# A cond-layernorm attention block on one core: SP stores the finished rows, residuals are kept in DRAM early, and TensorE sums two slabs where GpSimd summed one

## The chip, the cores and the metric

The kernel runs on one core of a Trainium2 chip. Its metric is the device time of one execution in microseconds (us), given as the median of several runs. The engines are TensorE (PE; its weight loads are PEld), VectorE (DVE), ScalarE (ACT), GpSimd (POOL) and SyncE (SP), which here only issues DMAs. Each engine runs its own list of instructions in order, and semaphores tie the lists together.

## The reference

`x` has 4 batches of 1024 tokens of 512 channels; there are 16 heads of 32 channels.

```
def _sln(h, w, ...):                       # layernorm with a gain and a bias from cond
    ln = (h - mu) / jnp.sqrt(var + EPS) * ln_g + ln_b
    return (w @ Wg.T + bg)[:, None, :] * ln + (w @ Wb.T + bb)[:, None, :]
h = _sln(hidden, w, ...)
qkv = (h @ Wqkv.T + bqkv).reshape(B, N, num_heads, hd, 3)
energy = jnp.einsum('bhqd,bhkd->bhqk', q, k)
att = jax.nn.softmax(energy, axis=-1) / D ** 0.5
out = jnp.einsum('bhqk,bhkd->bhqd', att, v)  ->  (B, N, D)
h1 = (out @ Wp.T + bp) + hidden
return _sln(h1, w, ...) + h1
```

## The kernel before

The 64 heads (4 batches by 16) are worked in 16 iterations of 4 heads; the 4096 tokens are 16 pairs of 128-token tiles. Every engine has a hand-written program in which an iteration is 32 steps, 8 for each head: step = 8 s + k, s the head in the iteration, k = 0 to 7. What an engine does at a step stands in small tables (`PAIR_ADD_STEP`, `NORM_SCALE_STEP`, `OUT_LOW_STEP` and so on). A step has no clock: an engine comes to it when its own list and its waits let it.

**One head.** TensorE makes the plain scores (ps_a, ps_w, or one bank of ps_st; L821), of which VectorE takes row maxima (L1367, `half_max`); the negated maxima are turned (L815), copied (L1374, L1376, `max_rows`), and SP stores them as two more rows of `q_stack` (`store_row`, L511, at k = 5 of the head before). Then TensorE makes the turned scores with the maximum already taken off (L835, ps_st) and ScalarE takes exp of them into eight slabs of 128x1024 (L1130; `p`, and `p_far` for every second head once it is free). TensorE multiplies the slabs with V (`weighted`, L852) in two halves of four slabs. The first turned score of the next head needs the row of `store_row` and stands at k = 7.

**The sum of the exponentials.** Of each half of four slabs VectorE adds slab 0 to slab 1 (`slab_add`, L1294), POOL adds slab 2 to slab 3 (`pair_add` with even j, L1658) and then slab 1 to slab 3 (odd j, same line). TensorE multiplies the one slab that is left with a constant (`chain_sum`, L865), at k = 0 of the next head for the first half and at k = 4 for the second. SP carries the sums to `sum_t` (`store_sums`, L527, k = 7), VectorE inverts them at step 9 (L1288) and SP stores them at step 10 (L533).

**Three kinds of iteration.** Iterations 0 to 10 ("tiles") also norm and project a pair of x tiles for a later batch: POOL scales it (`norm_scale` with `power`, steps 15 and 20; L1511 to L1523) and gives it gain and bias (`norm_gain`, steps 16 and 24). Iterations 11 to 14 ("bare") have no x tiles left, and iteration 15 ("last") has a list of its own. From iteration 4 on, each iteration also finishes a pair of output tiles ("outs"): SP loads `go_s` (gain and bias), the attention rows and the scales at step 14 and x itself into `res_t` at step 1 (`load_residual`, L554); POOL adds bp to it (`residual`, L1549), scales the rows (`out_norm`, L1539) and makes their low part (`out_low`, L1544); TensorE projects (L726, in bare iterations at steps 25 to 31), VectorE adds residual and projection (`out_sum`, L1303), and POOL norms, scales and adds in `out_scale` and `out_finish` (L1558 to L1570). `out_finish` ends with the store of the rows from POOL's own queue (L1572), at steps 3 and 11 of the next iteration. SP waits for the second `out_finish` before it loads the next `go_s` (step 14; step 5 in the last iteration). SP's list is strictly in order, so what stands behind that wait waits too.

`power` is eps + variance, minus the mean (L1512), a drain, the -0.5 power, a drain.

Of the kernel before, what the change touches and what calls it, by code (L numbers as in the profile page):

```python
# [72 lines left out]
RESIDUAL_BARE = {15: 0, 16: 1}  # L73
# [8 lines left out]
OUT_LOAD_STEP = 14  # L82


def conditioned_attention(nc, x, cond, ln_g, ln_b, Wg, bg, Wb, bb, Wqkv, bqkv, Wp, bp, out):
    B, N, D = x.shape
    HD = 32
# [15 lines left out]
    out_rows = out.rearrange("b n d -> (b n) d")  # L103

# [5 lines left out]
    mark_d = nc.dram_tensor("mark_scratch", [2, 1, 16], F32, kind="Internal").ap()  # L110
# [8 lines left out]
    with ExitStack() as ctx:  # L119
# [121 lines left out]
        res_ready = sem("res_ready")  # L241
        scale_in = [sem(f"scale_in{s}") for s in range(2)]
# [33 lines left out]
        LATE = END - 1  # L276
        PRE_LOAD_STEP = {11 + 2 * t: t for t in range(8)}
# [6 lines left out]
        ACC_ADD_STEP = {9: (0, 1), 10: (2, 3), 20: (4,), 22: (5,), 24: (6,), 26: (7,)}  # L284
        LATE_MM_STEP = {10: 0, 12: 1}
# [102 lines left out]
        SUM_SLOT = [3, 7]  # L388

# [39 lines left out]
        def _(sp):  # L429
# [198 lines left out]
            def iteration(i, tiles, norms, outs, first=False, last=False, gather=False):  # L628
                pair = i - FIRST_OUTS
                for s in range(4):  # L630
                    u = 4 * i + s
                    for k in range(8):
# [34 lines left out]
                        if last and step == 5:  # L667
# [24 lines left out]
            with sp.Fori(1, FIRST_OUTS) as i:  # L692
                iteration(i, True, True, False)
            with sp.Fori(FIRST_OUTS, LAST_TILES - 1) as i:
# [24 lines left out]
        def _(pe):  # L719
# [137 lines left out]
            def chain_sum(g, s, h, near=False):  # L857
# [199 lines left out]
        def _(act):  # L1057
# [61 lines left out]
            def exps(i, step, paired, tiles, behind):  # L1119
# [3 lines left out]
                                2: (pair_added, 4 * v + 2 * half + 1), 3: (sum_done, 2 * v + half + 1)}[k % 4 if paired else 3]  # L1123
                for e in range(2):
# [18 lines left out]
            def iteration(i, mode, outs, first=False, more=False, joining=False):  # L1143
                pair = i - FIRST_OUTS
                tiles, last = mode == "tiles", mode == "last"
                for step in range(32):
# [12 lines left out]
                    exps(i, step, paired, tiles, 1 if tiles or (joining and s == 0) else 2)  # L1159
# [46 lines left out]
        def _(dve):  # L1206
# [89 lines left out]
            def out_sum(pair, a):  # L1296
# [3 lines left out]
                dve.wait_ge(res_ready, P + 1)  # L1300
# [111 lines left out]
            def iteration(i, mode, norms, outs, first=False, late=True, closing=False, joining=False):  # L1412
                pair = i - FIRST_OUTS
                tiles, last = mode == "tiles", mode == "last"
                for s in range(4):
                    for k in range(8):
# [32 lines left out]
                        if outs:  # L1449
                            for a in sums:  # L1450
                                out_sum(pair, a)
# [38 lines left out]
        def _(pool):  # L1490
# [15 lines left out]
            for a in range(2):  # L1506
                G.dma_start(mark_d[a], ident[0:1, 0:16]).then_inc(y_out[a], 16)
# [9 lines left out]
            def norm_scale(pair, a):  # L1517
# [5 lines left out]
                G.tensor_scalar(h_tile[:, a, :], x_tile[:, a, :], std_t[:, a, 0:1], std_t[:, a, 1:2], ALU.add, ALU.mult  # L1523
# [26 lines left out]

            def out_scale(pair, a, count, gains=None):

                pool.wait_ge(out_stat, 2 * pair + a + 1)

# [3 lines left out]
                G.tensor_scalar(y, h1_t[:, a, :], ostd_t[:, a, 0:1], ostd_t[:, a, 1:2], ALU.add, ALU.mult  # L1558
# [5 lines left out]
            def out_finish(pair, a, count):  # L1564
# [6 lines left out]
                pool.wait_ge(out_pool, count + 5)  # L1571
                G.dma_start(out_rows[bass.ds((2 * pair + a) * 128, 128), :], y).then_inc(y_out[a], 16)  # L1572
# [18 lines left out]
            def last_iteration(i):  # L1591

                count = 10 * LATE + ONE
                for step in range(32):
# [158 lines left out]
```

## Time and profile before

| | |
|---|---|
| time, median of 3 runs | 1386.43 us (1386.4 to 1388.2) |
| the profiled execution: its time / its span | 1391.84 us / 1390.2 us |
| PE / POOL / DVE / ACT busy, of the span | 93% / 76% / 77% / 51% |
| mean granted TensorE clock | 0.97 |

Times in the rows below are counted from the start of the span. Busy time of PE is of overlapping matmuls, so a busy PE is not PE at its peak. A clock of 1.00 is 2.4 GHz, of 0.50 it is 1.2 GHz. POOL's, DVE's and PE's lists run at different steps at one time.

### The profile page before, as it was taken

Reading aid. Unit: us, or ns where it says so; the run is one execution under the profiler, and the core shown is the slowest. Engines: PE = TensorE matmul, PEld = TensorE weight load, DVE = VectorE, ACT = ScalarE, POOL = GpSimd, SP = SyncE. Lnnn points to the kernel's source line nnn. Section 1 sums busy time; section 2 is a strip of 40 time slices with the busy share of each in tenths; the row PEclk is TensorE's granted clock in tenths of the full one; section 3 lists DMA queues with packets and bytes.
Section 4 is the critical chain, followed back from the end, with each engine's and each line's share of the span. In section 5 each row is a group of like instructions: output and inputs, shape, how many; then the busy total and the mean of one; then the engine's idle time right before and its main releaser. Section 6 shows DMA issues by size and latency. Waiting matters only on the chain.

```text
span 1390.2 us, 33206 instructions
## 1 busy us (share of the span) xinstructions
PE 1294.5 (93%) x9988; PEld 904.0 (65%) x9988; DVE 1065.7 (77%) x1754; ACT 702.4 (51%) x1374; POOL 1062.6 (76%) x755
## 2 busy tenths in 40 slices
PE   7898999999999999999999999999989898989993
PEld 4897676767676767676776767677545555555562
DVE  5345788888888888787888878787968788887535
ACT  4221355555565556455555556555545555555341
POOL 1444176767676799899898999997897989898845
PEclk9899899999999999999999999999999999999997
DMA  7578534443444545446454635437453434243321
GB/s 245 144 209 228 126 94 115 116 115 107 106 122 109 150 116 162 105 144 152 125 148 114 174 93 159 105 116 159 123 134 84 116 84 113 83 114 92 89 55 64
DMA packets 216708, 174.13 MB, mean 125 GB/s; under 512 B 105493, under 2 KB 186517, under 8 KB 216633
## 3 DMA queue, kind: packets, MB, share of 16 engines
q1 hardware_dynamic: 214456, 166.83, 45.0%
q0 software_dynamic: 1984, 6.29, 1.2%
q8 instruction: 40, 0.66, 0.2%
q14 instruction: 36, 0.29, 0.1%
q10 hardware_dynamic: 192, 0.07, 0.0%
HBM read 113.29 MB, written 58.51 MB: 124 GB/s over the span
## 4 chain that ended last, share of the span: by engine, by line
PE 39%; POOL 27%; issue 17%; POOLq 6%; DVE 6%; DMA 2%; SPq 1%; ACT 1%; DVEq 1%; ACTq 0%
POOL p L1658 15%; PE ps_o L852 7%; PE ps_st L835 6%; PE ps_a L821 5%; PE ps_w L784 4%; PE ps_w L726 4%; POOLq L1513 4%; PE ps_st L784 3%; DVE half_max L1367 2%; PE ps_s L865 2%; POOL y_t L1568 2%; POOL p_far L1658 2%; POOLq L1515 2%; POOL y_t L1570 1%; POOL h_tile L1531 1%
## 5 line engine op out<-in xcount | busy, mean ns | idle before, releaser
L1130 ACT ACTIVATE p<-ps_st 128x512 f32<-128x512 f32 x864 | 485.8, 599 | 434.4 <-PE ps_st L835 395.4
L1658 POOL TENSOR_TENSOR p<-p 128x1024 f32<-128x1024 f32 x208 | 532.0, 2558 | 144.2 <-PE ps_o L852 133.7
L1367 DVE TENSOR_REDUCE half_max<-ps_a 128x1 f32<-128x512 f32 x729 | 483.5, 684 | 120.6 <-PE ps_a L821 116.8
L835 PE MATMUL ps_st<-q_stack,k_stack 98*128 98x512 f32 x1024 | 419.1, 411 | 8.5 <-ACT p L1130 3.5
L821 PE MATMUL ps_a<-k_stack,q_stack 96*128 96x512 f32 x729 | 310.2, 428 | 15.0 <-DVE half_max L1367 11.9
L835 PEld LDWEIGHTS ps_st<-q_stack,k_stack 98*128 98x128 f32 x1024 | 197.6, 193 | 70.3 <-ACT p L1130 39.8
L852 PE MATMUL ps_o<-p,v_head 128*32 128x256 f32 x3456 | 210.7, 384 | 0.0
L821 PEld LDWEIGHTS ps_a<-k_stack,q_stack 96*128 96x128 f32 x729 | 139.9, 193 | 94.5 <-issue 40.3
L1367 DVE TENSOR_REDUCE half_max<-ps_st 128x1 f32<-128x512 f32 x231 | 158.3, 685 | 29.3 <-PE ps_st L821 28.8
L784 PEld LDWEIGHTS ps_w<-hT_s,wqkv_s 128*128 128x128 f32 x1056 | 157.5, 190 | 20.2
L852 PEld LDWEIGHTS ps_o<-p,v_head 128*32 128x32 f32 x3456 | 110.9, 111 | 79.3 <-issue 7.2
L784 PE MATMUL ps_w<-hT_s,wqkv_s 128*128 128x256 f32 x1056 | 161.8, 281 | 0.0
L1294 DVE TENSOR_TENSOR p<-p 128x1024 f32<-128x1024 f32 x104 | 140.6, 1352 | 22.9 <-PE ps_o L852 19.6
L1130 ACT ACTIVATE p_far<-ps_st 128x512 f32<-128x512 f32 x160 | 88.9, 603 | 92.1 <-PE ps_st L835 91.6
L1658 POOL TENSOR_TENSOR p_far<-p_far 128x1024 f32<-128x1024 f32 x32 | 83.2, 2601 | 18.7 <-PE ps_o L852 17.1
L821 PE MATMUL ps_st<-k_stack,q_stack 96*128 96x512 f32 x231 | 95.4, 413 | 0.0
L726 PE MATMUL ps_w<-wqkv_s,hT_s 128*128 128x512 f32 x300 | 84.8, 395 | 0.0
L865 PE MATMUL ps_s<-p,root_s 128*32 128x256 f32 x832 | 66.3, 390 | 17.6 <-POOL p L1658 17.0
L726 PE MATMUL ps_w<-wp_s,oT_s 128*128 128x512 f32 x288 | 80.0, 397 | 0.1
L726 PEld LDWEIGHTS ps_w<-wqkv_s,hT_s 128*128 128x128 f32 x300 | 56.7, 189 | 13.5
L726 PEld LDWEIGHTS ps_w<-wp_s,oT_s 128*128 128x128 f32 x288 | 54.3, 189 | 13.3 <-POOL oT_s L1544 0.5
L1531 POOL TENSOR_TENSOR h_tile<-h_tile,gq_s 128x512 f32<-128x512 f32 x32 | 44.1, 1378 | 16.3 <-DMA gq_s<-gain_bias_scratch 13.5
(201 smaller groups left out, 1433.6 us busy)
## 6 DMA issues: line engine op xcount, KB each, us to landing
qk_scratch<-qkT_s SPq DMA_DIRECT2D x108, 256.0 KB, 2.4
q_stack<-qk_scratch SPq DMA_DIRECT2D x192, 128.0 KB, 2.6
k_stack<-qk_scratch SPq DMA_DIRECT2D x192, 128.0 KB, 2.8
x_tile<-in_x SPq DMA_DIRECT2D x34, 256.0 KB, 4.9
gq_s<-gain_bias_scratch SPq DMA_DIRECT2D x16, 512.0 KB, 4.2
v_scratch<-v_parts SPq DMA_DIRECT2D x32, 256.0 KB, 3.5
v_head<-v_scratch SPq DMA_DIRECT2D x64, 128.0 KB, 2.1
att_scratch<-o_stage SPq DMA_DIRECT2D x240, 32.0 KB, 1.5
```

Source lines behind the costliest of these rows:

```text
L726: mm = pe.matmul(dst, left[:, lp, c, :], right[:, rp, c, :], start=(n == 0), stop=(n == 11))
L784: mm = pe.matmul(bank[:, part * 256:(part + 1) * 256], wqkv_s[:, lp, w, d, chunk * 128:(chunk + 1) * 128], hT[:, rp, d, :], start=(n == 0) ...
L821: pe.matmul(A_BANK[bank], q_stack[0:96, s, t * 128:(t + 1) * 128], k_stack[0:96, s, half * 512:(half + 1) * 512], start=True, stop=True).t ...
L835: pe.matmul(ps_st[:, (ST_BANK_WIDE if wide else ST_BANK)[2 * k + e], :], k_stack[0:98, s, k * 128:(k + 1) * 128], q_stack[0:98, s, e * 512 ...
L852: mm = pe.matmul(ps_o[HD * e:HD * e + HD, 0:QW], v_head[:, s, k, :], p_of(s, near)[:, k, e * QW:(e + 1) * QW], start=(k == 0), stop=(k == 7))
L865: mm = pe.matmul(ps_s[HD * e:HD * e + HD, 0:QW], root_s[:], p_of(s, near)[:, SUM_SLOT[h], e * QW:(e + 1) * QW], start=(h == 0), stop=(h == 1))
L1130: nc.scalar.activation(p_of(step // 8, tiles)[:, k, e * 512:(e + 1) * 512], ps_st[:, (ST_BANK_WIDE if tiles else ST_BANK)[2 * k + e], :], ...
L1294: V.tensor_tensor(p[:, 4 * h + 1, :], p[:, 4 * h, :], p[:, 4 * h + 1, :], ALU.add).then_inc(slab_added, 1)
L1367: V.tensor_reduce(half_max[:, s % 2, item:item + 1], A_BANK[bank], AX.X, ALU.max).then_inc(a_used, 1)
L1513: pool.drain()
L1531: G.tensor_tensor(h, h, gq_s[:, 0, :], ALU.mult).then_inc(ln_pool, 1)
L1658: G.tensor_tensor(p[:, 4 * h + 3, :], p[:, 4 * h + 2 - j % 2, :], p[:, 4 * h + 3, :], ALU.add).then_inc(pair_added, 1)
```

## The change

1. **Stores.** `out_finish` loses its DMA. SP stores the rows instead: in iterations with outs at steps 6 and 13, in the last iteration at steps 8, 13, 22 and 28. (The two small DMAs to `mark_scratch` become semaphore increments.)
2. **Fused mean.** `power` loses the minus-the-mean instruction; the tensor_scalar behind it subtracts the mean and multiplies, where it added and multiplied.
3. **Kept residuals.** In iterations 1 to 4 POOL adds bp to two x tiles (`keep_residual`, steps 17 and 21) and SP stores the result in DRAM (steps 23 and 27). The pairs are 7 to 10. In iterations 11 to 14 SP loads these in place of x, and POOL adds no bp there; `out_sum` waits for the load itself.
4. **Sums.** In iterations 11 to 14 the odd `pair_add` is gone: POOL adds once a half head, and `chain_sum` multiplies two slabs (1 and 3) instead of one.
5. **Last iteration.** SP waits for `out_finish` and loads `go_s` at step 10 instead of 5, behind the store of the inverted sums; POOL adds bp to the last residuals at step 6, ahead of `finish_late`, instead of step 7 behind it.

```diff
-RESIDUAL_BARE = {15: 0, 16: 1}
+Y_STORE_STEP = {6: 0, 13: 1}
+KEEP_STEP = {17: 0, 21: 1}
+KEEP_STORE_STEP = {23: 0, 27: 1}
...
+        LATE_STORE_STEP = {8: (LATE - 1, 0), 13: (LATE - 1, 1), 22: (LATE, 0), 28: (LATE, 1)}
...
+            def store_y(pair, a):
+                sp.wait_ge(out_pool, 10 * pair + 5 * a + 5 + ONE)
+                sp.dma_start(out_pairs[bass.ds(pair, 1), a].rearrange("b p d -> (b p) d"), y_t[:, a, :]).then_inc(y_out[a], 16)
+            def store_kept(pair, a):
+                sp.wait_ge(res_kept, 2 * (pair - KEPT) + a + 1)
+                sp.dma_start(res_d[bass.ds(pair, 1), a].rearrange("b p d -> (b p) d"), y_t[:, a, :]).then_inc(kept_out[a], 16)
+            def load_kept(pair, a):
+                sp.wait_ge(kept_out[a], 16 * BARE)
+                sp.wait_ge(out_summed, 2 * pair + ONE)
+                sp.dma_start(res_t[:, a, :], res_d[bass.ds(pair, 1), a].rearrange("b p d -> (b p) d")).then_inc(res_in[a], 16)
...
+                        if outs and late and not last and step in Y_STORE_STEP:
+                            store_y(pair - 1, Y_STORE_STEP[step])
+                        if last and step in LATE_STORE_STEP:
+                            store_y(*LATE_STORE_STEP[step])
                         if outs and step == RESIDUAL_LOAD_STEP:
                             for a in range(2):
-                                load_residual(pair, a)
+                                if tiles or last:
+                                    load_residual(pair, a)
+                                else:
+                                    load_kept(pair, a)
+                        if keep and step in KEEP_STORE_STEP:
+                            store_kept(i + LEAD + 1, KEEP_STORE_STEP[step])
...
-                        if last and step == 5:
+                        if last and step == 10:
...
-                pe.wait_ge(pair_added, 16 * g + 4 * s + 2 * h + 2)
-                for e in range(4):
-                    mm = pe.matmul(ps_s[HD * e:HD * e + HD, 0:QW], root_s[:], p_of(s, near)[:, SUM_SLOT[h], e * QW:(e + 1) * QW],
-                                   start=(h == 0), stop=(h == 1))
+                slabs = [SUM_SLOT[h]] if near else [SUM_SLOT[h] - 2, SUM_SLOT[h]]
+                for n, slab in enumerate(slabs):
+                    if near:
+                        pe.wait_ge(pair_added, 16 * g + 4 * s + 2 * h + 2)
+                    elif n == 0:
+                        pe.wait_ge(slab_added, 8 * g + 2 * s + h + 1)
+                    else:
+                        pe.wait_ge(pair_added, 8 * g + 2 * s + 2 * FIRST_BARE + h + 1)
+                    for e in range(4):
+                        mm = pe.matmul(ps_s[HD * e:HD * e + HD, 0:QW], root_s[:], p_of(s, near)[:, slab, e * QW:(e + 1) * QW],
+                                       start=(h == 0 and n == 0), stop=(h == 1 and slab == SUM_SLOT[1]))
...
-                dve.wait_ge(res_ready, P + 1)
+                if mode == "bare":
+                    dve.wait_ge(res_in[a], 16 * pair + 16)
+                else:
+                    dve.wait_ge(res_ready, P + 1 - (2 * BARE if mode == "last" else 0))
...
-                G.tensor_tensor(std[:, 0:1], zero_s[:, 0:1], mv[:, 0:1], ALU.subtract)
...
+            def keep_residual(pair, a):
+                need(pool, kept_out[a], 16 * (pair - KEPT))
+                G.tensor_tensor(y_t[:, a, :], x_tile[:, a, :], bp_s[:], ALU.add).then_inc(res_kept, 1)
...
-                pool.wait_ge(out_pool, count + 5)
-                G.dma_start(out_rows[bass.ds((2 * pair + a) * 128, 128), :], y).then_inc(y_out[a], 16)
...
                     if step == 6:
                         for a in range(2):
                             out_low(LATE, a)
-                        finish_late(LATE - 1, 0)
-                    if step == 7:
-                        finish_late(LATE - 1, 1)
                         for a in range(2):
                             residual(LATE, a)
+                    if step == 7:
+                        finish_late(LATE - 1, 0)
+                        finish_late(LATE - 1, 1)
...
+                if j % 2 and not near:
+                    return
...
-                    if outs and step in (RESIDUAL_STEP if tiles else RESIDUAL_BARE):
-                        residual(pair, (RESIDUAL_STEP if tiles else RESIDUAL_BARE)[step])
+                    if keep and step in KEEP_STEP:
+                        keep_residual(ahead + 1, KEEP_STEP[step])
+                    if outs and tiles and step in RESIDUAL_STEP:
+                        residual(pair, RESIDUAL_STEP[step])
```

## Rows read from the trace of the kernel before

**Rows 1.** Stages (`windows`): us, busy of PE, PEld, DVE, ACT, POOL; clock, DMA share, GB/s.

```profile
709.80:787.30 77.50, 75.40 (x606) 54.59 (x605) 64.32 (x108) 42.97 (x85) 71.28 (x51) 1.00 0.51 136
...
1152.90:1223.06 70.16, 63.30 (x478) 38.00 (x476) 59.34 (x92) 37.83 (x75) 63.15 (x38) 0.95 0.38 98
```

**Rows 2.** TensorE's timeline: sums (L865) that waited for POOL in tiles iterations.

```profile
344.18 0.64 PE L865 MATMUL ps_s<-p,root_s 128*32 128x256 f32 x8 [0.20 <-POOL p L1658]
...
722.47 0.64 PE L865 MATMUL ps_s<-p,root_s 128*32 128x256 f32 x8 [1.22 <-POOL p L1658]
```

**Rows 3.** POOL's timeline ahead of the first and the last of these sums.

```profile
339.26 4.87 POOL L1658 TENSOR_TENSOR p<-p 128x1024 f32<-128x1024 f32 x2
...
704.95 0.63 POOL L1572 DMA_DIRECT2D out_y<-y_t  x1 [0.68 <-POOL y_t L1570]
...
712.04 0.18 POOL L1512 TENSOR_TENSOR std_t<-zero_s,mv_t 128x1 f32<-128x1 f32 x1
```

**Rows 4.** Groups of POOL's instructions, whole span: busy us, mean ns, idle before.

```profile
L1549 POOL TENSOR_TENSOR res_t<-res_t,bp_s 128x512 f32<-128x512 f32 x24 | 32.1, 1346 | 0.2
```

**Rows 5.** Iteration 13 head by head (`windows`, cut where SP issues each `store_row`).

```profile
1134.64:1148.73 14.09, 13.89 (x120) 7.89 (x113) 13.22 (x22) 8.86 (x18) 12.69 (x11) 1.00 0.36 91
1148.73:1169.88 21.15, 16.05 (x121) 9.62 (x113) 15.67 (x21) 9.20 (x19) 20.21 (x12) 0.84 0.57 138
1169.88:1187.24 17.36, 16.54 (x133) 10.17 (x125) 15.37 (x22) 10.43 (x20) 15.03 (x7) 1.00 0.23 62
```

**Rows 6.** TensorE's timeline, iteration 12: the sums that waited in the long head.

```profile
1080.34 0.64 PE L865 MATMUL ps_s<-p,root_s 128*32 128x256 f32 x8 [1.29 <-POOL p L1658]
...
1090.96 0.64 PE L865 MATMUL ps_s<-p_far,root_s 128*32 128x256 f32 x8 [3.50 <-POOL p_far L1658]
```

**Rows 7.** The chain that ended last, in a bare iteration: start, us, what.

```profile
1197.62 0.43 PE ps_s L865 x8
```

**Rows 8.** SP's timeline, iteration 13, step 13 to step 21.

```profile
1148.73 1.47 SPq L511 DMA_DIRECT2D q_stack<-max_rows  x2
1154.39 0.37 SPq L432 DMA_DIRECT2D go_s<-gain_bias_scratch  x1
...
1168.35 0.38 SPq L504 DMA_DIRECT2D v_head<-v_scratch  x1
1169.88 1.46 SPq L511 DMA_DIRECT2D q_stack<-max_rows  x2
```

**Rows 9.** TensorE's timeline: turned scores that waited for the stored row.

```profile
1030.85 0.80 PE L835 MATMUL ps_st<-q_stack,k_stack 98*128 98x512 f32 x1 [0.93 <-DMA q_stack<-max_rows]
...
1103.29 0.50 PE L835 MATMUL ps_st<-q_stack,k_stack 98*128 98x512 f32 x1 [1.03 <-DMA q_stack<-max_rows]
```

**Rows 10.** Stretches right behind stalls of TensorE (`windows`).

```profile
1161.20:1167.00 5.80, 5.72 (x19) 3.95 (x20) 3.23 (x5) 2.68 (x6) 5.72 (x5) 0.51 0.78 179
...
1091.00:1095.00 4.00, 4.00 (x17) 2.81 (x18) 2.35 (x4) 2.05 (x4) 4.00 (x3) 0.60 0.48 106
1231.40:1239.00 7.60, 7.59 (x25) 5.38 (x25) 5.11 (x9) 4.31 (x8) 7.52 (x5) 0.55 0.73 169
...
1018.00:1023.00 5.00, 4.92 (x24) 2.90 (x24) 3.78 (x8) 3.57 (x8) 4.86 (x4) 1.00 0.79 184
```

**Rows 11.** Timelines of SP, VectorE and TensorE in the last iteration.

```profile
1288.68 0.36 SPq L432 DMA_DIRECT2D go_s<-gain_bias_scratch  x1
...
1294.18 0.35 DVE L1288 RECIPROCAL rcp_t<-sum_t 128x32 f32<-128x32 f32 x1 [8.21 <-issue]
...
1295.14 0.50 PE L821 MATMUL ps_a<-k_stack,q_stack 96*128 96x512 f32 x1 [2.99 <-DVE half_max L1367]
1296.40 1.80 PE L852 MATMUL ps_o<-p_far,v_head 128*32 128x256 f32 x16
```

**Rows 12.** Timelines of SP and TensorE, iteration 7: step 21's row, and its reader.

```profile
722.94 1.44 SPq L511 DMA_DIRECT2D q_stack<-max_rows  x2
...
729.78 0.40 PE L835 MATMUL ps_st<-q_stack,k_stack 98*128 98x512 f32 x1
```

More of the change, by code:

```diff
@@ L103, in conditioned_attention @@
     out_rows = out.rearrange("b n d -> (b n) d")
+    out_pairs = out_rows.rearrange("(t a p) d -> t a p d", a=2, p=128)
     qk_d = nc.dram_tensor("qk_scratch", [4, B, D, N], F32, kind="Internal").ap()
@@ L241, in conditioned_attention @@
         res_ready = sem("res_ready")
+        res_kept = sem("res_kept")
+        kept_out = [sem(f"kept_out{a}") for a in range(2)]
         scale_in = [sem(f"scale_in{s}") for s in range(2)]
@@ L276, in conditioned_attention @@
         LATE = END - 1
+        KEPT = LAST_TILES - FIRST_OUTS
+        BARE = LAST - LAST_TILES
         PRE_LOAD_STEP = {11 + 2 * t: t for t in range(8)}
@@ L388, in conditioned_attention @@
         SUM_SLOT = [3, 7]
+        FIRST_BARE = 4 * LAST_TILES
         def p_of(v, near):
@@ L626, in _, with iteration @@
                 store_v(LEAD - 1, a)
-            def iteration(i, tiles, norms, outs, first=False, last=False, gather=False):
+            def iteration(i, tiles, norms, outs, first=False, last=False, gather=False, late=True, keep=False):
                 pair = i - FIRST_OUTS
@@ L692, in _ @@
             with sp.Fori(1, FIRST_OUTS) as i:
-                iteration(i, True, True, False)
-            with sp.Fori(FIRST_OUTS, LAST_TILES - 1) as i:
+                iteration(i, True, True, False, keep=True)
+            iteration(FIRST_OUTS, True, True, True, late=False, keep=True)
+            with sp.Fori(FIRST_OUTS + 1, LAST_TILES - 1) as i:
                 iteration(i, True, True, True)
@@ L1117, in pre_split, with exps @@
                 nc.scalar.activation(oT_s[:, t % 2, 0, 0:DC - 1], att_t[:, t % 2, 0:DC - 1], ACT.Copy).then_inc(pre_high, 1)
-            def exps(i, step, paired, tiles, behind):
+            def exps(i, step, paired, tiles, behind, chained):
                 n, k = 64 * i + 2 * step, step % 8
@@ L1123, in exps @@
                                 2: (pair_added, 4 * v + 2 * half + 1), 3: (sum_done, 2 * v + half + 1)}[k % 4 if paired else 3]
+                if paired and not chained and k % 4 == 1:
+                    freed, count = sum_done, 2 * v + half + 1
+                elif paired and not chained and k % 4 == 2:
+                    freed, count = pair_added, 2 * v + 2 * FIRST_BARE + half + 1
                 for e in range(2):
@@ L1158, in iteration @@
                         act.wait_ge(tile_mm, 8 * PAIRS)
-                    exps(i, step, paired, tiles, 1 if tiles or (joining and s == 0) else 2)
+                    exps(i, step, paired, tiles, 1 if tiles or (joining and s == 0) else 2, tiles or (joining and s < 2))
                     if more and step - 1 in NEXT_TURNED:
@@ L1450, in iteration @@
                             for a in sums:
-                                out_sum(pair, a)
+                                out_sum(pair, a, mode)
                                 if last:
@@ L1522, in norm_scale @@
                 power(mv_t[:, a, :], std_t[:, a, :], ln_pool)
-                G.tensor_scalar(h_tile[:, a, :], x_tile[:, a, :], std_t[:, a, 0:1], std_t[:, a, 1:2], ALU.add, ALU.mult
+                G.tensor_scalar(h_tile[:, a, :], x_tile[:, a, :], mv_t[:, a, 0:1], std_t[:, a, 1:2], ALU.subtract, ALU.mult
                                 ).then_inc(ln_pool, 1)
@@ L1557, in out_scale @@
                 y = y_t[:, a, :]
-                G.tensor_scalar(y, h1_t[:, a, :], ostd_t[:, a, 0:1], ostd_t[:, a, 1:2], ALU.add, ALU.mult
+                G.tensor_scalar(y, h1_t[:, a, :], omv_t[:, a, 0:1], ostd_t[:, a, 1:2], ALU.subtract, ALU.mult
                                 ).then_inc(out_pool, 1)
@@ L1679, in finish_late, with iteration @@
                     out_finish(pair, 1, count)
-            def iteration(i, mode, norms, outs, first=False, late=True, joining=False):
+            def iteration(i, mode, norms, outs, first=False, late=True, joining=False, keep=False):
                 pair = i - FIRST_OUTS
@@ L1715, in _ @@
             with pool.Fori(1, FIRST_OUTS) as i:
-                iteration(i, "tiles", True, False)
-            iteration(FIRST_OUTS, "tiles", True, True, late=False)
+                iteration(i, "tiles", True, False, keep=True)
+            iteration(FIRST_OUTS, "tiles", True, True, late=False, keep=True)
             with pool.Fori(FIRST_OUTS + 1, LAST_TILES - 1) as i:
```

7 lines of the change are left out of this document (4 added, 3 removed).

## The prediction

> **What bounds the kernel now.** I read the page for the shares of busy time, then the stages, the chain of waits, and the timelines of TensorE, POOL and SP around each wait that the chain names.
>
> In tiles iterations TensorE is the bound: 75.4 of 77.5 us busy at full clock, POOL 71.3 [rows 1]. What is left to win there is the few sums that wait for POOL [rows 2]. In bare iterations TensorE has less work (63.3 busy of 70.2 us) and POOL, at 63.2 plus its DMA issues, drains and waits, is nearly full [rows 1]. By heads, the loss is in one place: the head from step 5 to 13 takes 14.1 us, the next, with no more TensorE work, 21.15, at a mean clock of 0.84 [rows 5]. Two sums wait there for POOL, 1.29 and 3.50 us in iteration 12 [rows 6], and behind such a stall TensorE runs some us at about half clock [rows 10]. The head of 17.4 us and the one behind it hold the two output projections. They and the short head are set by TensorE and VectorE together: 13.9 and 13.2 us busy of 14.1 [rows 5].
>
> In the last iteration SP stands at step 5 until `out_finish` is over and issues `go_s` at 1288.68; the sums of the head before stand behind it in SP's queue. VectorE waits 8.21 us for them before its inversion, TensorE 2.99 us for VectorE, and its next 16 products take 1.80 us [rows 11].
>
> **The change, part by part.**
>
> *Stores and fused mean, tiles iterations.* The sum at 722.47 waits 1.22 us, and one step before it another waits 0.20 us like that at 344.18 [rows 2]. POOL is busy without a break from 686 to that sum. The change takes out of this stretch a DMA (0.68 us wait for the last add, 0.63 issue) and two minus-the-means (each 0.15 start to start, 0.18 long) [rows 3]: 1.6 us, more than the 1.42 that TensorE waits. So 1.42 us for each of iterations 5 to 9, where it recurs: -7.1 us. If TensorE finds another wait it is 0; more than 9 us isn't there.
>
> *Kept residuals, iterations 1 to 4.* An add of 128x512 is 1.35 us on the mean, with contention [rows 4]; alone it is about 1.28, and I take that. The one at step 17 stands between the two adds of 4.87 us for which the sum at 344.18 already waits 0.20 us [rows 2, 3]. So nothing hides it: 1.28 less the 0.15 of the fused mean is 1.13 us, four times, +4.5 us. The one at step 21 stands where POOL was idle before, and has some 2 us of room. From below the cost is 0, if the first was only late by chance; from above 2 x 1.35 x 4 = 10.8. What the bare iterations get back for it is counted with them.
>
> *Sums, bare iterations.* Eight more records at 0.43 us a half head [rows 7] are 0.87 us a head for TensorE. VectorE is idle at the end of that block already, so I take it in full; 0.64 us, the length of the group in the timeline [rows 6], is the upper bound. Against it, POOL loses 8 adds of 2.4 us, two of 1.3 and two DMAs of 1.3 an iteration, 25 us of 70. Both waits of rows 6 go, and POOL isn't the bound any more. What is late next? By TensorE alone the long head would become 14.1 + 0.87 = 14.95 us. But SP: in iteration 13 it stood 4 us before `go_s` and then issued without a break from 1154.39 to 1168.73, 14.3 us, and the row of step 21 could go out 0.2 us later [rows 8]. This work isn't less; one store comes before it. With the row of step 13 (1.47 us), a store (0.45, like the loads of its size) and the gaps, `go_s` can start 2.55 us after the row of step 13, and the row of step 21 goes out at 2.55 + 14.55 = 17.1 us. In iteration 12 SP needed 1 us more; I take 17.6. TensorE has no slack for that row: at 1103.29 it waited 1.03 us for one [rows 9]. So a wait for the row takes the place of the wait for POOL. An iteration: head 5 to 13 +0.87; 13 to 21 17.6 - 21.15 = -3.55; 21 to 29 +0.87, +0.15 for the later row; 29 to 37 +0.87. Together -0.8 us; for iterations 12 to 14, -2.4. In iteration 11 three more loads (x for the last tiles) stand in SP's queue and the stall on the row is there already [rows 9]; I take it as unchanged.
>
> The clock: stalls of 3.5 us and less were followed by 4 to 7.6 us at 0.51 to 0.60, which cost 5.8 x 0.49 = 2.8, 4.0 x 0.40 = 1.6 and 7.6 x 0.45 = 3.4 us, mean 2.6; but behind one of 3.3 us the clock stayed 1.00 [rows 10], and behind 1.22 us too. The new stall is some 2.7 us. I take half of 2.6, three times: +3.9 us; from below 0, from above 10. Bare iterations in all: +1.5 us.
>
> This is where a rule weighs against the change. The Trainium skill, Perfetto Trace Analysis, section DMA Optimizations, says that where the issuing of DMAs is the bottleneck one should balance them over the engines that can issue, and perhaps give outputs an engine of their own. Before, the outputs had one (POOL). SP's unbroken 14.3 us agrees that issuing binds there; by that rule SP without the store would be 0.65 us earlier in this head, some 2.6 us in the four iterations.
>
> *Last iteration.* The inversion no longer stands behind `out_finish`: the sums can leave SP at about 1278 and be there at 1282, when VectorE comes to them at 1286. TensorE's 2.99 us go, and most of the slow stretch: 1.80 us for 16 products that take 1.07 at full clock, and as much again for the sums behind them [rows 11]. -4.7 us. The moved bp adds take 2.6 us of POOL, and the missing add gives 2.4 back, so `out_finish` comes no later and only `go_s` waits for it. Four stores of SP there stand between loads that TensorE needs later; nothing. If the stretch is slow anyway, -3.
>
> Start, end, the smaller DMAs: nothing; the work beside them is longer.
>
> **Sum**: -7.1 + 4.5 + 1.5 - 4.7 = -5.8 us. It is made on an execution of 1391.8 us (span 1390.2); the median of the runs is 1386.4, 5.4 less, and I take the difference off that: 1380.6 us.
>
> **Rivals.**
>
> *B, SP has room.* If SP issues faster with POOL's DMAs gone, the long head takes 14.95 us, the row isn't late, the clock stays. 2.8 us an iteration for three, the 3.9 of the clock, and some 6 for iteration 11: 18.3 us less, 1362.3. For it: SP stood idle 4 us in that head. Against: its 14.3 us are without a break, and in iteration 12 the row was late with SP already 4 us less pressed.
>
> *C, the clock falls after every stall for the row.* +3.9 us, 1384.5, within 0.2% of before. For: three stretches of four [rows 10]. Against: the stall is shorter than the sum of the two before.
>
> *D, slower: SP late in tiles iterations too.* There the row of step 21 is issued at 722.94 and read at 729.78 [rows 12]; landing takes it to 726.5, so 3.3 us of room. TensorE comes 1.4 us earlier and SP 0.65 later: 1.2 left. If it is missed by 1 us in iterations 5 to 9 and the clock falls for the shortest of the stretches (1.6), 5 x 2.6 = 13 us: 1393.6. It decides from 1.8 us an iteration on. For: SP is busy there without a break as well. Against: the room is more than any landing in that stretch varied by.
>
> *E, nothing won in tiles iterations*, since each sum comes back behind some other add: 1380.6 + 7.1 = 1387.7.
>
> **How the numbers follow.** Forecast 0.43, B 0.20, C 0.15, D 0.12, E 0.10. The range takes in B to nearly D: 1362 to 1391; the forecast's own is 1374 to 1384. A measurement of this kernel tells 0.2%, 2.8 us, from no change. Faster (under 1383.7): forecast nearly whole, B, a part of C: 0.67. Same: C and E mostly: 0.18. Slower: D and the bad end of E: 0.15.
>
> **What would show it.** Sums (L865) that wait for POOL should be gone in iterations 5 to 14 and be longer by 1.1 us once in each of iterations 1 to 4. The head from step 13 to 21 of bare iterations should be 17 to 18 us, with a turned score that waits for the stored row, and SP without a break before it. The other three heads should be longer by 0.9 us. VectorE's inversion in the last iteration should wait for nothing. The prediction is wrong if the turned scores don't wait for the row, if the sums cost TensorE more than 0.64 us, or if the clock falls in iterations where it did not.

## The result, and the profile after

The changed kernel takes 1393.64 us (median of 6 runs, 1391.05 to 1395.25), the kernel before 1387.32 us on the same chip: a ratio of 1.0041, 95% interval 1.0028 to 1.0055. It is slower by 0.4%; the forecast was 1380.6 and its range ended at 1391. The profiled execution took 1393.59 us, its span is 1391.8 us, mean clock 0.976.

I cut each span where SP stores the inverted sums (step 10 of iterations 1 to 15), so that the stages can be compared (differences of starts in SP's timeline, us). The third column is the changed kernel with the old mean, an experiment of the next section ("mean unfused"):

| stage | before | after | mean unfused |
|---|---|---|---|
| start to iteration 1 | 249.2 | 248.6 | 246.9 |
| iterations 1 to 5 (residuals are kept) | 292.2 | 304.7 | 297.9 |
| 5 to 10 (tiles with outs) | 389.5 | 392.8 | 384.5 |
| 10 to 15 (bare) | 363.7 | 346.3 | 343.3 |
| 15 to the end | 95.6 | 99.3 | 99.1 |
| span | 1390.2 | 1391.8 | 1371.6 |

The stages "10 to 15" and "15 to the end" have to be read together: in the kernel before, the store of the inverted sums in iteration 15 was itself late [rows 11], so that the first of them was too long there and the second too short. Cut at SP's row of step 5 instead (in iteration 15 at 1275.77 before and 1281.54 after), iterations 11 to 14 won 10.0 us (284.3 to 274.3) and the last one 4.1 (114.4 to 110.3). Iterations 1 to 10 lost 16. POOL is where to look. First its groups over the whole span in the kernel before (busy us, mean ns of one | idle before):

```profile
L1523 POOL TENSOR_SCALAR h_tile<-x_tile,std_t 128x512 f32<-128x512 f32 x32 | 26.0, 814 | 6.2 <-issue 6.2
L1558 POOL TENSOR_SCALAR y_t<-h_t,ostd_t 128x512 f32<-128x512 f32 x24 | 18.4, 768 | 4.7 <-issue 4.7
```

and the same groups after:

```profile
L1571 POOL TENSOR_SCALAR h_tile<-x_tile,mv_t,std_t 128x512 f32<-128x512 f32 x32 | 69.6, 2174 | 6.2 <-issue 6.2
L1612 POOL TENSOR_SCALAR y_t<-h_t,omv_t,ostd_t 128x512 f32<-128x512 f32 x24 | 49.9, 2078 | 4.6 <-issue 4.6
```

The one instruction that the fused mean changes takes 2.7 times as long: 75.1 us more of POOL over the span. TensorE's waits tell what became of it; before (waited for: us in total, times, longest us):

```profile
PE ps_s L865 <- POOL p L1658: 17.0, 23, 1.8
PE ps_s L865 <- POOL p_far L1658: 13.8, 4, 3.5
```

and after:

```profile
PE ps_s L907 <- POOL p L1712: 26.3, 26, 2.0
PE ps_st L870 <- DMA q_stack<-max_rows: 6.8, 4, 3.2
```

The four long waits of the bare iterations (`p_far`) are gone, as forecast [rows 6]; the waits of the tiles iterations, which should have gone [rows 2], have grown. In iteration 7 there are three, in TensorE's timeline after:

```profile
724.73 0.64 PE L907 MATMUL ps_s<-p,root_s 128*32 128x256 f32 x8 [0.52 <-POOL p L1712]
...
735.46 0.64 PE L907 MATMUL ps_s<-p,root_s 128*32 128x256 f32 x8 [1.49 <-POOL p L1712]
...
746.31 0.64 PE L907 MATMUL ps_s<-p,root_s 128*32 128x256 f32 x8 [0.66 <-POOL p L1712]
```

2.67 us in place of 1.42 (before there is a second small wait of 0.20 beside the 1.22). In POOL's timeline after, the scale of the output rows and what follows it:

```profile
704.82 0.19 POOL L1560 TENSOR_TENSOR ostd_t<-omv_t,eps_s 128x1 f32<-128x1 f32 x1
705.15 0.56 POOL L1562 TENSOR_TENSOR ostd_t<-ostd_t,minus_half 128x1 f32<-128x1 f32 x1
705.90 2.08 POOL L1612 TENSOR_SCALAR y_t<-h_t,omv_t,ostd_t 128x512 f32<-128x512 f32 x1 [0.19 <-issue]
```

The minus-the-mean is gone between the first two (0.15 us), and the third takes 1.3 us more than its 0.77 before.

In iterations 1 to 4 the wait is 2.00 us each time, and behind three of the four TensorE's clock fell (windows right behind the waits of iterations 1 to 4; us, busy of PE, PEld, DVE, ACT, POOL, then clock):

```profile
273.45:277.50 4.05, 4.05 (x41) 1.96 (x41) 1.25 (x2) 1.08 (x2) 2.73 (x3) 0.58 0.43 67
348.92:353.00 4.08, 4.08 (x41) 1.90 (x42) 1.25 (x2) 1.08 (x2) 2.73 (x4) 0.60 0.43 66
424.27:428.30 4.03, 4.03 (x47) 2.63 (x48) 2.47 (x4) 1.97 (x4) 3.69 (x4) 1.00 0.44 67
498.06:502.10 4.04, 4.04 (x41) 2.05 (x42) 1.23 (x1) 1.08 (x2) 3.71 (x4) 0.61 0.46 74
```

The third kept its clock, and its iteration is the one that lost less: 1.7 us against 3.5, 3.4 and 3.9 of the others.

The bare iterations did what the change says. Iteration 13 head by head, after (answers to [rows 5]):

```profile
1148.77:1163.77 15.00, 14.74 (x137) 8.42 (x129) 14.01 (x22) 8.85 (x18) 13.06 (x8) 1.00 0.32 87
1163.77:1180.56 16.79, 16.60 (x159) 9.70 (x149) 14.32 (x23) 9.22 (x19) 9.65 (x5) 1.00 0.58 167
1180.56:1197.00 16.44, 15.13 (x119) 9.68 (x121) 12.52 (x21) 9.75 (x19) 6.69 (x4) 1.00 0.28 73
1197.00:1215.16 18.16, 17.38 (x149) 10.88 (x145) 15.27 (x26) 9.24 (x18) 12.18 (x8) 1.00 0.32 87
```

The long head has lost 4.4 us and POOL is busy for 9.65 us of it, where it was for 20.21. SP's timeline of that head, after (answers to [rows 8]):

```profile
1163.77 1.47 SPq L520 DMA_DIRECT2D q_stack<-max_rows  x2
1165.51 0.36 SPq L563 DMA_DIRECT2D out_y<-y_t  x1
1166.17 0.35 SPq L441 DMA_DIRECT2D go_s<-gain_bias_scratch  x1
...
1180.05 0.38 SPq L513 DMA_DIRECT2D v_head<-v_scratch  x1
1180.56 1.46 SPq L520 DMA_DIRECT2D q_stack<-max_rows  x2
```

SP issues without a break, and the head is as long as SP needs. The reader of the row, in TensorE's timeline after, waits:

```profile
1183.28 0.49 PE L870 MATMUL ps_st<-q_stack,k_stack 98*128 98x512 f32 x1 [0.77 <-DMA q_stack<-max_rows]
```

In iterations 11 and 12 this wait was 2.07 and 3.25 us, and behind both the clock was 0.51 and 0.50 for 6 us; behind 0.77 and 0.74 (iterations 13 and 14) it stayed 1.00.

### The profile page after: what moved, and what is told of

It reads as the page before. It is cut to its first block, busy times and chain, and to the rows that moved or that the text cites. A ratio compares the mean times of both kernels' runs of the same rounds, so it can differ in the third digit from the quotient of the medians.

```text
span 1391.8 us, 33477 instructions
## 1 busy us (share of the span) xinstructions
PE 1300.8 (93%) x10244; PEld 907.1 (65%) x10244; DVE 1050.3 (75%) x1754; ACT 700.4 (50%) x1374; POOL 1026.9 (74%) x641
## 4 chain that ended last, share of the span: by engine, by line
PE 43%; POOL 21%; issue 14%; DVE 7%; SPq 5%; POOLq 4%; DMA 2%; ACT 1%; DVEq 1%; ACTq 0%
POOL p L1712 13%; PE ps_o L887 9%; PE ps_st L870 7%; PE ps_a L856 6%; PE ps_w L761 6%; DVE half_max L1416 3%; PE ps_w L819 3%; PE ps_s L907 3%; POOLq L1561 3%; PE ps_st L819 2%; POOL h_tile L1571 2%; POOL h_tile L1579 2%; PE ps_st L856 2%; PE ps_w L942 1%; DVE p L1340 1%
## 5 line engine op out<-in xcount | busy, mean ns | idle before, releaser
L1712 POOL TENSOR_TENSOR p<-p 128x1024 f32<-128x1024 f32 x192 | 490.2, 2553 | 165.6 <-PE ps_o L887 158.0
L856 PE MATMUL ps_a<-k_stack,q_stack 96*128 96x512 f32 x729 | 306.4, 423 | 9.5 <-DVE half_max L1416 7.4
L870 PEld LDWEIGHTS ps_st<-q_stack,k_stack 98*128 98x128 f32 x1024 | 195.8, 192 | 75.1 <-ACT p L1176 40.3
L887 PE MATMUL ps_o<-p,v_head 128*32 128x256 f32 x3456 | 214.3, 389 | 0.0
L819 PEld LDWEIGHTS ps_w<-hT_s,wqkv_s 128*128 128x128 f32 x1056 | 157.0, 189 | 20.2
L1340 DVE TENSOR_TENSOR p<-p 128x1024 f32<-128x1024 f32 x104 | 132.5, 1274 | 35.6 <-PE ps_o L887 32.6
L907 PE MATMUL ps_s<-p,root_s 128*32 128x256 f32 x960 | 73.6, 391 | 26.3 <-POOL p L1712 26.3
L1712 POOL TENSOR_TENSOR p_far<-p_far 128x1024 f32<-128x1024 f32 x16 | 44.6, 2789 | 64.3 <-PE ps_o L887 64.3
L1571 POOL TENSOR_SCALAR h_tile<-x_tile,mv_t,std_t 128x512 f32<-128x512 f32 x32 | 69.6, 2174 | 6.2 <-issue 6.2
```

Source lines behind the costliest of these rows:

```text
L819: mm = pe.matmul(bank[:, part * 256:(part + 1) * 256], wqkv_s[:, lp, w, d, chunk * 128:(chunk + 1) * 128], hT[:, rp, d, :], start=(n == 0) ...
L856: pe.matmul(A_BANK[bank], q_stack[0:96, s, t * 128:(t + 1) * 128], k_stack[0:96, s, half * 512:(half + 1) * 512], start=True, stop=True).t ...
L870: pe.matmul(ps_st[:, (ST_BANK_WIDE if wide else ST_BANK)[2 * k + e], :], k_stack[0:98, s, k * 128:(k + 1) * 128], q_stack[0:98, s, e * 512 ...
L887: mm = pe.matmul(ps_o[HD * e:HD * e + HD, 0:QW], v_head[:, s, k, :], p_of(s, near)[:, k, e * QW:(e + 1) * QW], start=(k == 0), stop=(k == 7))
L1340: V.tensor_tensor(p[:, 4 * h + 1, :], p[:, 4 * h, :], p[:, 4 * h + 1, :], ALU.add).then_inc(slab_added, 1)
L1571: G.tensor_scalar(h_tile[:, a, :], x_tile[:, a, :], mv_t[:, a, 0:1], std_t[:, a, 1:2], ALU.subtract, ALU.mult).then_inc(ln_pool, 1)
```

## The experiments

Each was timed beside runs of the kernel before on the same chip; where no interval stands it is one run. "Unfused" is the first experiment's kernel, from which most of the others start.

**1. The changed kernel with the mean unfused.**

```diff
                 G.tensor_tensor(std[:, 1:2], mv[:, 1:2], eps_s[:, 0:1], ALU.add)
+                G.tensor_tensor(std[:, 0:1], zero_s[:, 0:1], mv[:, 0:1], ALU.subtract)
...
-                G.tensor_scalar(h_tile[:, a, :], x_tile[:, a, :], mv_t[:, a, 0:1], std_t[:, a, 1:2], ALU.subtract, ALU.mult
+                G.tensor_scalar(h_tile[:, a, :], x_tile[:, a, :], std_t[:, a, 0:1], std_t[:, a, 1:2], ALU.add, ALU.mult
```

(and the same for `y_t`).

> The changed kernel with one part undone: the minus-the-mean instruction is back in power, and the tensor_scalar adds and multiplies again. Theory S (the subtracting tensor_scalar of POOL is what made the kernel slower: 2.17 and 2.08 us in the changed kernel, 0.81 and 0.77 before): these instructions fall back to 0.8 us, an iteration of kind tiles with outs falls from 78.7 to about 76.2 us, one of iterations 1 to 3 from 73.6 to 75.5 down to about 73.1, and the time is 16 to 24 us below the changed kernel, 1370 to 1378, below the kernel before. Rival K (the kept residuals and the stores on SP made it slower, the long tensor_scalar lies beside other work): within 4 us of the changed kernel, about 1393.

Measured: 1374.01 us, ratio 0.9905 (0.9889 to 0.992), span 1371.6: 20.2 us less than after, by the table 1.7 before iteration 1, 6.8 in iterations 1 to 5, 8.4 in 5 to 10, 3.1 in the bare ones, 0.2 at the end. The time lies in the range expected for theory S. One wait for POOL is left in each of iterations 5 to 9, in TensorE's timeline:

```profile
722.08 0.64 PE L907 MATMUL ps_s<-p,root_s 128*32 128x256 f32 x8 [0.91 <-POOL p L1713]
```

The fused mean alone makes a change of +0.4% out of one of -1%.

**2. The fused mean alone, on the kernel before.** The edit of experiment 1 in the other direction.

> The kernel before with the fused mean alone. Theory S: each of the 56 tensor_scalars costs POOL 1.3 us more less 0.15, and where POOL is waited for (iterations 5 to 14) one or two of them an iteration reach the end of the sum: slower by 10 to 25 us, 1397 to 1412. Rival K: one instruction less, faster by 0 to 3 us.

Measured: 1423.76 us, ratio 1.0252 (1.0236 to 1.0267). The direction is right and the size, 35 us, is well above the 10 to 25 that I had expected. Half of it lies in the bare iterations: 380.1 us from iteration 10 to 15 against 363.7. There POOL was nearly full [rows 1], with the adds of the old sums. In iteration 13 the long head hardly grew (21.28 us for 21.15); the head behind it did, from 17.4 to 20.8 us.

**3. Add in place of subtract, operands of the changed kernel.** `ALU.subtract` becomes `ALU.add` in both tensor_scalars, nothing else (the mean is added, not taken off).

> The changed kernel with the tensor_scalar adding where it subtracted, its two scalars still from two tiles, so that the mean is added instead of taken off and the output isn't the reference's. If the operation is what costs: about 0.8 us for the instruction and a time like the kernel with the mean unfused. If it is the scalars from two tiles: 2.1 us and a time like the changed kernel.

**4. Subtract with both scalars in one tile, on the kernel before.** `power` copies the mean (mean minus zero), and the tensor_scalars subtract it.

> The kernel before with the same number of instructions: power copies the mean beside the power instead of minus the mean, and the tensor_scalar subtracts it, both scalars in one tile. If the operation is what costs: 2.1 us for the instruction, slower than before by 10 us or more. If it is the two tiles: 0.8 us and the time of before.

Measured, one run each: 1368.05 us for experiment 3 and 1433.5 us for experiment 4. The groups of 3:

```profile
L1571 POOL TENSOR_SCALAR h_tile<-x_tile,mv_t,std_t 128x512 f32<-128x512 f32 x32 | 27.4, 856 | 6.2 <-issue 6.2
L1612 POOL TENSOR_SCALAR y_t<-h_t,omv_t,ostd_t 128x512 f32<-128x512 f32 x24 | 18.5, 772 | 4.6 <-issue 4.6
```

and of 4:

```profile
L1523 POOL TENSOR_SCALAR h_tile<-x_tile,std_t 128x512 f32<-128x512 f32 x32 | 67.6, 2112 | 6.2 <-issue 6.2
L1558 POOL TENSOR_SCALAR y_t<-h_t,ostd_t 128x512 f32<-128x512 f32 x24 | 49.9, 2079 | 4.7 <-issue 4.7
```

It is the operation that costs, not the two tiles from which the scalars come. The span of 3 is 1366.3 us against 1371.6 unfused: one instruction less a row tile would be worth some 5 us, if what is left is an add (two profiles, and 3 computes another function).

**5. Unfused, without the kept residuals.** The bare iterations load x again and POOL adds bp to it, as before.

```diff
-                        if keep and step in KEEP_STORE_STEP:
-                            store_kept(i + LEAD + 1, KEEP_STORE_STEP[step])
...
-                if mode == "bare":
-                    dve.wait_ge(res_in[a], 16 * pair + 16)
-                else:
-                    dve.wait_ge(res_ready, P + 1 - (2 * BARE if mode == "last" else 0))
+                dve.wait_ge(res_ready, P + 1)
...
-                    if keep and step in KEEP_STEP:
-                        keep_residual(ahead + 1, KEEP_STEP[step])
-                    if outs and tiles and step in RESIDUAL_STEP:
-                        residual(pair, RESIDUAL_STEP[step])
+                    if outs and step in (RESIDUAL_STEP if tiles else RESIDUAL_BARE):
+                        residual(pair, (RESIDUAL_STEP if tiles else RESIDUAL_BARE)[step])
```

> On the kernel with the mean unfused (ratio 0.9905 to before), the kept residuals undone: POOL adds bp in iterations 11 to 14 again, nothing is kept in iterations 1 to 4. Theory L (the kept residuals only lose: 1.15 us in each of iterations 1 to 3 and 2.4 in iteration 4, and POOL has room in the bare iterations now): 5 us faster, ratio 0.986 to 0.988. Rival G (they pay in the bare iterations, since POOL is still waited for there): within 2 us or slower, 0.990 or more.

Measured: 1367.38 us, ratio 0.9838 (0.9812 to 0.9864). Iterations 1 to 5 take 292.1 us against 297.9 unfused, the bare iterations 343.4 against 343.3. Keeping the residuals cost 5.7 us in the profiles and gave nothing back: with one add a half head POOL has the room for bp itself. The ratio is lower than expected (0.986 to 0.988), by more than these 5.7 us; the rest is open.

**6. Unfused, with sums of one slab as before.** POOL adds twice a half head again.

> On the kernel with the mean unfused, the sums of iterations 11 to 14 as before: POOL adds twice a half head, TensorE multiplies one slab. If taking the adds off POOL is worth what the long head showed: iterations 12 to 14 go back from 66 to 69 us to about 69 to 70, and the time is 5 to 10 us above, ratio 0.994 to 0.998. If POOL without its stores and residuals had room for them anyway, TensorE's 0.87 us a head come back and it is up to 10 us faster, ratio 0.983 to 0.990.

Measured: 1386.44 us, ratio 0.9972 (0.9957 to 0.9987). The bare iterations take 354.1 us against 343.3. In TensorE's timeline of iteration 13 the wait for POOL is back, and the wait for the row stands beside it:

```profile
1158.43 0.64 PE L900 MATMUL ps_s<-p_far,root_s 128*32 128x256 f32 x8 [1.26 <-POOL p_far L1700]
1171.54 0.79 PE L870 MATMUL ps_st<-q_stack,k_stack 98*128 98x512 f32 x1 [2.04 <-DMA q_stack<-max_rows]
```

and behind the second the clock is half (window):

```profile
1171.60:1177.00 5.40, 5.40 (x31) 3.13 (x35) 2.26 (x4) 2.39 (x4) 3.26 (x3) 0.50 0.53 138
```

The sums of two slabs are what wins, 10.8 us in the profiles; the ratio is in the range expected.

**7. Unfused, rows stored by POOL.** `out_finish` ends with its DMA again and SP's stores go.

> On the kernel with the mean unfused, the rows stored by POOL again. My terms: 0.6 us in each of iterations 6 to 9 and 2.6 in iteration 5 are lost, and SP's later row in iterations 11 to 14 (it waits 0.7 to 1.9 us) gives back up to 0.65 each: 2 to 4 us slower, ratio 0.992 to 0.994. Rival (SP's queue is what counts): 2 us faster or more, 0.989 or less.

Measured: 1372.97 us, ratio 0.9872 (0.9849 to 0.9895), against 0.9905 (0.9889 to 0.992) with SP's stores: the intervals just overlap, and the value is that of the rival (0.989 or less) and not mine. In the profiles iterations 5 to 10 take 387.2 us against 384.5, the bare ones 340.7 against 343.3. SP's stores win in one stage what they lose in the other. But of the 2.6 us of the bare ones 1.9 lie between the stores of iterations 11 and 12, where the wait for the row is 1.59 us with a clock of 0.71 behind it, against 1.89 and 0.50; in the last two stages, where the clock stays 1.00, the gain is 0.2 us each.

**8. Unfused, last iteration in the old order.**

```diff
-                        if last and step == 10:
+                        if last and step == 5:
...
                             out_low(LATE, a)
-                        for a in range(2):
-                            residual(LATE, a)
+                        finish_late(LATE - 1, 0)
                     if step == 7:
-                        finish_late(LATE - 1, 0)
                         finish_late(LATE - 1, 1)
+                        for a in range(2):
+                            residual(LATE, a)
```

> On the kernel with the mean unfused, the last iteration in its old order: SP waits for out_finish and loads go_s at step 5, POOL adds bp behind finish_late. Theory: VectorE's inversion waits for the sums behind SP's wait again, TensorE 2 to 3 us for it, and then a slow stretch: 3 to 6 us slower, ratio 0.993 to 0.995. Rival (POOL has less to do ahead of it now, so that SP is not held): no change, 0.990.

Measured: 1375.16 us, ratio 0.9898 (0.9876 to 0.992): the order makes no difference here. The inversion does come later and waits again, in VectorE's timeline:

```profile
1276.88 0.35 DVE L1334 RECIPROCAL rcp_t<-sum_t 128x32 f32<-128x32 f32 x1 [5.16 <-DMA sum_t<-o_stage]
```

but TensorE, which waited 2.99 us behind it before [rows 11], waits for at most 0.41. In SP's timeline the load of `go_s` is no longer as late as it was [rows 11]:

```profile
1261.08 1.58 SPq L520 DMA_DIRECT2D q_stack<-max_rows  x2
1271.29 0.37 SPq L441 DMA_DIRECT2D go_s<-gain_bias_scratch  x1
```

10.2 us behind the row, where it was 12.9 (1275.77 to 1288.68) before. POOL, without its second adds, is through with `out_finish` earlier.

**9. Sums alone.** The kernel before with part 4 of the change and nothing else.

> The kernel before with the two-slab sums of the bare iterations alone: POOL stores the rows, the mean has its own instruction, no residual is kept, the last iteration has its old order. Theory 'the sums carry nearly all of the gain': bare iterations as where POOL stored the rows (71.2, 68.7, 68.5, 66.1, 66.2 us from one store of inverted sums to the next, against 70.8, 72.8, 70.1, 70.3, 79.6 before), tiles iterations unchanged at 77.6, so a span of 1370 to 1373 and a ratio of 0.985 to 0.988. Rival 'the sums need SP's stores, since POOL is else the bound': bare iterations stay above 70 us and the ratio above 0.992.

Measured: 1369.96 us, ratio 0.9873 (0.985 to 0.9895). The ratio is in the range of the theory. The stages behind the start take 292.2, 389.7, 349.4 and 94.3 us; the last two are to be read together here too (15.7 us less than before), since the last store of inverted sums is late again in the old order. One of five parts is worth more than the five together.

**10. Stores by stage, no kept residuals.** SP stores the rows in tiles iterations, POOL from iteration 11 on, with a semaphore of its own.

```diff
-                        if outs and late and not last and step in Y_STORE_STEP:
+                        if outs and late and tiles and step in Y_STORE_STEP:
...
-            def out_finish(pair, a, count):
+            def out_finish(pair, a, count, pooled=False):
...
+                if pooled:
+                    pool.wait_ge(out_pool, count + 5)
+                    G.dma_start(out_rows[bass.ds((2 * pair + a) * 128, 128), :], y).then_inc(y_pool[a], 16)
```

> The version without kept residuals (unfused mean, two-slab sums, new last order), in which SP stores the rows only in tiles iterations and POOL stores them from iteration 11 on. Theory 'SP's stores win 0.6 us in a tiles iteration and lose in bare ones, where SP issues without a break': tiles iterations 76.95 us as with SP's stores, the turned scores' wait for the row of step 21 shorter by 1 to 2 us in iterations 11 and 12 and gone in 13 and 14, bare iterations together 2 to 3 us shorter than in the version without kept residuals; ratio 0.981 to 0.983. Rival 'who stores makes no difference': ratio 0.984 to 0.986 and the same waits for the row.

Measured: 1364.83 us, ratio 0.9837 (0.9813 to 0.9861), the fastest here, though not apart from experiment 5 (0.9838). Tiles iterations take 384.5 us as with SP's stores, the bare ones 341.3, 2.1 less than in experiment 5. The ratio lies between the theory (0.981 to 0.983) and the rival (0.984 to 0.986). Iteration 13, the head from step 13 to 21 and the next:

```profile
1138.16:1154.37 16.21, 16.02 (x157) 9.23 (x147) 14.08 (x22) 9.22 (x19) 11.55 (x7) 1.00 0.64 173
1154.37:1171.15 16.78, 15.96 (x121) 10.06 (x124) 12.87 (x21) 9.76 (x19) 7.28 (x4) 1.00 0.26 71
```

The first is 0.6 us shorter than with SP's store, and the wait for the row has shrunk from 0.84 us (experiment 5) to 0.20; the second gives 0.4 of it back. In iteration 12 the wait is 1.66 us and the clock behind it 0.50; in iteration 11 it is 1.99 us and the clock stays 1.00, where in experiment 5 it was 0.71 behind 2.17 us. That is where most of the 2.1 us comes from: 1.8 lie between the stores of iterations 11 and 12 (67.6 us against 69.4), and only 0.2 and 0.3 in each of the last two stages. Nothing here shows that the place of the stores decided the clock.

**11. Unfused, multiply first.** `h_tile` is multiplied and then added to, `y_t` is multiplied and then subtracted from (so another function is computed).

> The changed kernel with the mean unfused, but both tensor_scalars have other operations in the same shapes: h_tile is multiplied and then added to, y_t is multiplied and then subtracted from (the output is of another computation). Theory 'a subtract anywhere in a tensor_scalar of POOL costs': h_tile 0.77 us, y_t 2.1 us a piece. Rival 'only a subtract in first place costs': both 0.77 us. Rival 'only add first is fast': both 2.1 us.

Measured (1380.19 us), the groups of POOL:

```profile
L1613 POOL TENSOR_SCALAR y_t<-h_t,ostd_t 128x512 f32<-128x512 f32 x24 | 49.9, 2078 | 4.6 <-issue 4.6
L1572 POOL TENSOR_SCALAR h_tile<-x_tile,std_t 128x512 f32<-128x512 f32 x32 | 24.6, 769 | 6.2 <-issue 6.2
```

A subtract costs in the second place as in the first; an add in neither.

## Why the prediction was wrong

**The step that failed** is "Stores and fused mean": it took 0.15 us off for each minus-the-mean and gave the changed tensor_scalar no term at all, as if it kept its 0.77 us. There was no row of a tensor_scalar with a subtract, and I bounded the term from neither side. It measured 2.08 to 2.17 us on the mean, 56 times. TensorE got 20.2 us of it in the profiles (experiment 1), and without it the change is faster: 0.9905. That is also what decided the sign. The Trainium skill, GPSIMD Engine Reference, section Elementwise — side-by-side cycle accounting, gives 768 ns for a loop over 512 elements at best; the trace agrees for add and multiply (means of 768 to 856 ns) and not for subtract, for which the page has no figure.

That term is not the whole miss. With the mean unfused the profile is 18.6 us under before, where the other steps were to give 5.8: they were far too careful, in the bare iterations above all, and the two errors partly cancelled in the time. The other steps are measured on the unfused kernel against before, stage by stage:

| step | forecast | measured |
|---|---|---|
| stores and fused mean, iterations 5 to 9 | -7.1 | -5.0 |
| kept residuals, iterations 1 to 4 | +4.5 | +5.7 |
| bare iterations and last iteration | +1.5 - 4.7 | -16.9 |
| start | 0 | -2.3 |
| sum | -5.8 | -18.6 |

The -2.3 of the start is within what that stretch varies by between profiles (last section).

**Tiles iterations.** Of the -5.0, 2.6 fall between the stores of iterations 5 and 6; each of the other four stages won 0.6 us, not 1.42. The wait is 0.91 us where it was 1.22. POOL's work did come 1.5 us earlier, but then its adds met VectorE's, which they had missed before. POOL and VectorE, unfused:

```profile
705.59 5.85 POOL L1713 TENSOR_TENSOR p<-p 128x1024 f32<-128x1024 f32 x2
...
704.91 1.80 DVE L1340 TENSOR_TENSOR p<-p 128x1024 f32<-128x1024 f32 x1
```

and in the kernel before:

```profile
707.06 4.87 POOL L1658 TENSOR_TENSOR p<-p 128x1024 f32<-128x1024 f32 x2
...
704.72 1.22 DVE L1294 TENSOR_TENSOR p<-p 128x1024 f32<-128x1024 f32 x1
```

Both are longer where they overlap: 1.0 us comes back on POOL. It is so in the whole profile of the unfused kernel: from 500 us on, the 16 pairs of adds with no slab add of VectorE beside them take 4.84 to 4.93 us, those with 1.1 us of one beside them 5.85 to 5.91. (The Trainium skill, SBUF — State Buffer, section Who interferes with whom, says that a VectorE instruction with two inputs in SBUF contends with a GpSimd instruction that reads SBUF; these rows agree.) That was rival E, "each sum comes back behind some other add", in part. Keeping the two apart was not tried.

**Kept residuals.** The mechanism held: TensorE's wait in iterations 1 to 3 is 1.31 us unfused, and the price is 1.0 to 1.2 us an iteration, 2.4 in the fourth (4.1 in the profiles of experiments 6 and 8, which keep residuals too and where the clock fell behind the second of its two waits). That the bare iterations gain nothing for it (experiment 5) I had not said.

**Sums.** TensorE's part was right: the short head takes 14.96 us (forecast 14.95). SP's was right too: in iteration 13 it issues without a break, the row goes out 16.8 us behind the last (worked out 17.1, taken 17.6). Two sizes were off. The head from step 21 to 29 was to be 18.4 us and is 16.4: before, it carried TensorE's arrears from the stall, 133 products [rows 5] where it now has 119, though a head's sums are 16 products more, and these I had counted as its own work. And in iterations 13 and 14 the wait is 0.7 to 0.8 us, not 2.7, and the clock doesn't fall; in 11 and 12 it does (1.8 to 1.9 us unfused, clock 0.50 and 0.70 behind them). Counted from SP's row of step 5 to the next one, iterations 11 to 14 so take 70.4, 69.0, 66.3 and 66.3 us unfused, against 73.0, 70.1, 70.3 and 70.8 before.

**Last iteration.** From the row of step 5 to the end it is 110.1 us unfused against 114.4 before, -4.3 where -4.7 was forecast, and the inversion waits for nothing, but the cause is not the order alone. Either of the two edits does it beside SP's stores and the kept residuals: the new order with the old sums (experiment 6, 109.7 us) and the old order with the new sums (experiment 8, 110.2 us). The new sums do most of it with no other part of the change (experiment 9, 111.2 us).

**The rivals.** D (SP late in tiles iterations) names almost the measured time, 1393.6, and that is luck: it did not come, since no turned score there waits for its row, before or after. B (SP has room) is wrong as put, since SP had none, but right in that iterations 13 and 14 win 4.0 and 4.5 us and keep their clock. C (the clock falls behind every stall for the row) came in two of the four, the long ones. The Trainium skill's rule on balancing the DMAs over the engines (Perfetto Trace Analysis, section DMA Optimizations) I had priced at 0.65 us earlier for the row, 2.6 us in four iterations. Experiment 10 beside experiment 5 agrees on the row (the wait is 0.64 us shorter in iteration 13) and not on the sum: an iteration whose clock stays gains 0.2 to 0.3 us, and the rest of its 2.1 us goes with the clock of one iteration.

## What to carry to other kernels

An edit that removes an instruction by giving its work to a neighbour changes the neighbour's operation: look for a row of the new operation, and where there is none, measure it by itself first or bound it above by something slow. Take the parts of a change one by one: here the sums alone (0.9873) beat the five parts together (1.0041), and the fastest kernel here (0.9837) leaves two of the parts out and keeps a third for one stage only. Work that moves off a full engine is worth only what the next engine, here SP with its unbroken list, lets through, and it can be paid for in a stage where the first engine was full as well.

## What the runs showed of the hardware

- On GpSimd a tensor_scalar of 128x512 f32 with a subtract in either place takes 2.08 to 2.17 us on the mean, with add and multiply 0.77 to 0.86 us. A tensor_tensor has no such gap: the subtract that makes the low part (`out_low`) takes 1.28 us on the mean in the unfused kernel, like the adds of that size beside it (1.28 to 1.30).
- A pair of 128x1024 adds on GpSimd takes 4.87 us, and 5.85 us where a slab add of VectorE lies over 1.1 us of it; VectorE's own add goes from 1.22 to 1.80 us.
- The stretch up to the first store of inverted sums takes 246.5 to 254.2 us in the profiles, by kernels that are mostly alike there. Differences of spans under some 4 us are read from the later stages only.
- A stall of one length need not do to the clock what another did: behind 2.00 us it was 0.58, 0.60, 1.00 and 0.61; behind 0.8 us, and behind the waits of 1.2 to 1.3 us for POOL in iterations 1 to 4 (unfused), it stayed 1.00. Behind the second of two waits of 1.21 us in iteration 4 it was 1.00 unfused, but 0.58 and 0.57 in experiments 6 and 8. Of the waits for a row, those of 1.32 (experiment 7), 1.66, 1.81, 1.89, 2.04, 2.07, 3.02 (experiment 5) and 3.25 us were followed by 0.50 to 0.71, and one of 1.99 us by 1.00. In the kernel before, the clock that stayed 1.00 behind 3.28 us [rows 10] fell behind the next wait, one of 0.93 us for a row [rows 9], which the prediction does not count among its slow stretches (window right behind it):

```profile
1031.00:1037.00 6.00, 6.00 (x35) 3.39 (x39) 2.93 (x4) 2.39 (x4) 4.87 (x4) 0.50 0.48 135
```
